# A two-layer graph network on one Trainium2 core: 128-row indirect transfers with three skipped rows in place of 125-row ones

## The reference

```
    h = jnp.maximum(_layernorm(x, axis=-1), 0.0)
    x = x + _L0_gnn_ref(h, edge_attr_2, weight, root_w, root_b, edge_index)
    h = jnp.maximum(_layernorm(x, axis=-1), 0.0)
    x = x + _L1_gnn_ref(h, edge_index, W_gat, att_src, att_dst, ...)

    # L0: messages = einsum('ek,ei,kio->eo', basis, x[row], weight)
    #     out = zeros.at[col].add(messages) / max(degree, 1) + x @ root_w.T + root_b
    # L1: alpha = leaky_relu(a_src[src] + a_dst[dst]); softmax over each dst, self loop included
    #     out = segment_sum(xp[src] * attn, dst).mean(heads) + bias
    #     h = layer_norm(out + x); layer_norm(relu(h @ w1 + b1) @ w2 + b2 + h)
```

## Time and profile before

| | us |
|---|---|
| median of 3 runs | 3408.22 (3392.78 to 3413.61) |
| the profiled execution, own time | 3399.81 |
| its span | 3398.0 |
| POOL busy | 2533.3 (75%) |
| PE busy | 2270.3 (67%) |
| DVE busy | 1842.4 (54%) |
| ACT busy | 862.2 (25%) |

### The profile page before, as it was taken

One profiled execution on the slowest core, in us unless ns is written; L12 is line 12 of the kernel. 1 busy time (PEld: TensorE's weight loads), 2 busy tenths in 40 slices (PEclk: granted clock), 3 DMA queues, 4 the chain that ended last, 5 costly groups with the idle time before them and its releaser, 6 DMA issues.

```text
span 3398.0 us, 34863 instructions
## 1 busy us (share of the span) xinstructions
PE 2270.3 (67%) x10329; PEld 1608.8 (47%) x10329; DVE 1842.4 (54%) x3167; ACT 862.2 (25%) x1636; POOL 2533.3 (75%) x2011
## 2 busy tenths in 40 slices
PE   2886777747777777777777475566561587887750
PEld 1554455535555555565555354445440244454430
DVE  4788878883433434333333232322248998797730
ACT  1332222212333232322323122222221122222220
POOL 7788888887887878787777787887840038888877
PEclk9888888877888787777877676676665798787775
DMA  2322222221111112121111111111100001111100
GB/s 57 85 70 70 68 71 65 48 63 31 33 38 35 38 37 41 36 41 35 38 27 32 26 24 24 24 27 20 23 16 0 30 15 29 32 26 28 33 10 10
DMA packets 116073, 123.70 MB, mean 36 GB/s; under 512 B 70597, under 2 KB 72618, under 8 KB 115941
## 3 DMA queue, kind: packets, MB, share of 16 engines
q0 software_dynamic: 64000, 30.57, 9.4%
q1 hardware_dynamic: 51940, 91.52, 8.4%
HBM read 59.51 MB, written 64.00 MB: 36 GB/s over the span
## 4 chain that ended last, share of the span: by engine, by line
POOL 65%; issue 19%; DVE 8%; PE 7%; DMA 0%; DVEq 0%; ACT 0%; POOLq 0%; ACTq 0%
POOL ring L409 44%; POOL x_table L431 14%; POOL out_rows L457 6%; DVE region L1457 2%; PE V L773 1%; PE C L525 1%; PE V L513 1%; DVE region L1449 1%; DVE region L1123 1%; DVE region L1433 1%; DVE region L1385 0%; PE C L773 0%; DVE region L1408 0%; DVE region L1405 0%; PE C L519 0%
## 5 line engine op out<-in xcount | busy, mean ns | idle before, releaser
L409 POOL DMA_INDIRECT ring<-in_x,index x800 | 1042.6, 1303 | 244.3 <-issue 244.0
L457 POOL DMA_INDIRECT out_rows<-ring,index_out x400 | 510.0, 1275 | 370.3 <-DVE ring L1264 250.6
L1092 DVE TENSOR_REDUCE var<-sq 125x16 f32<-125x512 f32 x325 | 220.4, 681 | 839.9 <-ACT sq L838 734.9
L409 POOL DMA_INDIRECT ring<-x_table,index x400 | 492.0, 1230 | 124.4 <-issue 124.1
L431 POOL DMA_INDIRECT x_table<-region,index_out x400 | 485.7, 1214 | 121.9 <-issue 121.9
L838 ACT ACTIVATE sq<-C 125x512 f32<-125x512 f32 x300 | 179.4, 598 | 961.9 <-PE C L525 416.5
L513 PE MATMUL V<-xT,w_q 128*128 128x500 f32 x600 | 365.3, 762 | 53.5 <-ACT xT L830 25.7
L474 PE MATMUL T<-ident,hrow 125*128 125x125 f32 x1000 | 196.3, 335 | 194.4 <-DVE hrow L1108 171.8
L525 PEld LDWEIGHTS C<-w_c,hid 128*125 128x125 f32 x2400 | 320.1, 219 | 0.0
L525 PE MATMUL C<-w_c,hid 128*125 128x32 f32 x2400 | 319.4, 296 | 0.0
L489 PE MATMUL C<-center,xT 128*125 128x128 f32 x1400 | 258.6, 347 | 78.5 <-DVE hrow L1114 47.2
(11 more groups left out here) (223 smaller groups left out, 3421.6 us busy)
## 6 DMA issues: line engine op xcount, KB each, us to landing
ring<-in_x,index POOLq DMA_INDIRECT x800
nodes<-in_x SPq DMA_DIRECT2D x25, 500.0 KB
x_table<-nodes SPq DMA_DIRECT2D x25, 500.0 KB
x_plain<-nodes SPq DMA_DIRECT2D x25, 500.0 KB
nodes<-x_plain SPq DMA_DIRECT2D x50, 250.0 KB
out_rows<-nodes SPq DMA_DIRECT2D x50, 250.0 KB
x_table<-region,index_out POOLq DMA_INDIRECT x400
ring<-x_table,index POOLq DMA_INDIRECT x400
```

Of the source, the lines that this page charges most:

```text
L409: pool.indirect_dma_start(out=ring[0:P, j, s * F:(s + 1) * F], out_offset=None, in_=table, in_offset=bass.IndirectOffsetOnAxis(ap=index[0: ...
L457: pool.indirect_dma_start(out=out[:, :], out_offset=bass.IndirectOffsetOnAxis(ap=index_out[0:P, j, s:s + 1], axis=0), in_=ring[0:P, j, s * ...
L1092: v.tensor_reduce(unit(var, k), slots(squares(k)), AX.X, ALU.add).then_inc(var_ready, 1)
```

## The change

Every indirect transfer now covers ROWS = 128 partitions. The last three rows of `index` and `index_out` are set to N = 100,000 by DVE at the start, and the gathers get the bounds check of the scatters, with `last_row` = N - 1: a row whose number is beyond it is skipped. Rows 125 to 127 of `ring` hold the bias; their load is moved from the end of SP's boot loads to their front, so N_BOOT falls by one. SP waits for DVE's two memsets before its first index load, and POOL waits for the bias before its first gather. DVE also clears rows 96 to 127 of the part of `region2` from which the scatters of `scatter_x1` now read three rows more.

```diff
-N_BOOT = 6 * 4 + 2 + 2 + 2 + 4
+N_BOOT = 6 * 4 + 2 + 2 + 2 + 3
...
+ROWS = 128
...
+            sp.dma_start(ring[P:128, :, :].rearrange("a j (s f) -> a (j s) f", f=F),
+                         root_b.rearrange("(a b f) -> a b f", a=1, b=1).to_broadcast([128 - P, NJ * CE, F])).then_inc(root_b_in, 16)
+            sp.wait_ge(index_set, 2)
             for j in range(NJ):
                 index_load(src, 0, j, None)
...
-            load(ring[P:P + 1, :, :].rearrange("a j (s f) -> a (j s) f", f=F),
-                 root_b.rearrange("(a b f) -> a b f", a=1, b=1).to_broadcast([1, NJ * CE, F]))
...
                     pool.indirect_dma_start(
-                        out=ring[0:P, j, s * F:(s + 1) * F], out_offset=None, in_=table,
-                        in_offset=bass.IndirectOffsetOnAxis(ap=index[0:P, j, s:s + 1], axis=0)).then_inc(ring_dma[j], 16)
+                        out=ring[0:ROWS, j, s * F:(s + 1) * F], out_offset=None, in_=table,
+                        in_offset=bass.IndirectOffsetOnAxis(ap=index[0:ROWS, j, s:s + 1], axis=0),
+                        bounds_check=last_row, oob_is_err=False).then_inc(ring_dma[j], 16)
...
+            pool.wait_ge(root_b_in, 16)
             gather_phase(x[:, :], 0, 0)
...
-                        out=x1_table[:, :], out_offset=bass.IndirectOffsetOnAxis(ap=index_out[0:P, j, s:s + 1], axis=0),
-                        in_=rows_out[0:P, j, s * F:(s + 1) * F], in_offset=None,
+                        out=x1_table[:, :], out_offset=bass.IndirectOffsetOnAxis(ap=index_out[0:ROWS, j, s:s + 1], axis=0),
+                        in_=rows_out[0:ROWS, j, s * F:(s + 1) * F], in_offset=None,
                         bounds_check=last_row, oob_is_err=False).then_inc(rows_landed[j], 16)
...
+            pool.wait_ge(index_set, 2)
...
-                            out=out[:, :], out_offset=bass.IndirectOffsetOnAxis(ap=index_out[0:P, j, s:s + 1], axis=0),
-                            in_=ring[0:P, j, s * F:(s + 1) * F], in_offset=None,
+                            out=out[:, :], out_offset=bass.IndirectOffsetOnAxis(ap=index_out[0:ROWS, j, s:s + 1], axis=0),
+                            in_=ring[0:ROWS, j, s * F:(s + 1) * F], in_offset=None,
                             bounds_check=last_row, oob_is_err=False).then_inc(ring_dma[j], 16)
...
+            v.memset(index[96:128, :, :], N).then_inc(index_set, 1)
+            v.memset(index_out[96:128, :, :], N).then_inc(index_set, 1)
+            v.memset(region2[96:128, 5904 + KS * GF:2 * H * TE + NJ * W], 0.0)
```

More of the change, by code:

```diff
@@ L195, in gnn_program @@
         VE = [V[0], V[1], C[1], T[1]]
+        index_set = sem("index_set"); root_b_in = sem("root_b_in")
         edges_in = sem("edges_in"); ends_in = sem("ends_in")
```

## The result

The changed kernel took **4504.05 us** (median of 4 runs, 4474.84 to 4532.82), the kernel before 3401.25 us in the same comparison (4 runs, 3392.78 to 3413.61): a ratio of 1.324, with an interval of 1.314 to 1.334. It is a third slower. The prediction said 2990 us, and its range ended at 3390.

The account below looks back on a forecast made before the run. POOL's indirect transfers were taken to bound the kernel outside the softmax stage. Gains of 66 + 165 + 92 + 97 - 2 = 418 us from the median of 3408 gave 2990 us, range 2770 to 3390.

Parts of the forecast that it names:

- Rival C: All 2,000 transfers: POOL's time goes with the rows, three more cost 29 ns, +58 us; 3468 us, chance 9%.
- Layout of the transfers: Each 125-row transfer runs on 5 engines with 25 rows each; 128 rows would spread evenly over 16, 8 each.
- Time of a transfer: POOL's indirect transfers: 0.98 us each, a saving of 0.23 us, with the 0.30 us gap unchanged.
- The check costs nothing, 26 us to both sides: Bounds check on 1,200 gathers: taken as free, with 1,200 x 0.022 = 26 us either way.
- Start-up: Boot loads: bias load and memset waits delay the first gather by 2 us, bound +5; -2 us in the sum.
- Landing: Gathered rows: spread over 16 engines they land sooner, a few us at most; nothing was taken.
- First pass: First source gather: a block falls from 133.2 to 116 us, DVE's 109.8 being the limit; 66 us in all.
- Second pass: Destination gather and table scatter: 720 transfers x 0.23 = 165 us; a block becomes 203 us, above PE's 178.
- Third pass: Second source gather: 400 x 0.23 = 92 us; a block becomes 105 us, far above PE's 77.
- Output pass: Output scatter: blocks fall to 112 us, saving 50 us, plus 47 us in the last stretch; together 97 us.
- POOL's backlog: Last stretch of output scatters: 113 left instead of 124, at 1.26 us; 142 instead of 189 us, saving 47 us.
- Rival A: Transfers of 0.85 us or less: POOL stops being the bound and other engines' floors decide; 2790 us, chance 17%.

Follow-up runs that it names:

- plain128: Changed kernel with no check and no skipped row in its 1,200 gathers, bias from its own tile; 4619.03 us, ratio 1.356, on chip 6.
- gathers128_b: Changed kernel with its 800 scatters back at 125 rows, repeated on chip 14: 3947.78 us, ratio 1.162; the same kernel took 3252.05 us on chip 4.
- rows120: Kernel before with 120-row indirect transfers, the last five of 125 rows left out, no check in the gathers: 3191.67 us.
- rows112: Kernel before with 112-row indirect transfers, rows 112 to 124 left out, no check in the gathers: 3171.21 us on chip 10.
- rows100: Kernel before with 100-row indirect transfers, the last 25 rows left out, no check in the gathers: 3208.09 us.
- skip112: Changed kernel with 112-row transfers whose last four rows are skipped, in all five passes: 3189.68 us on chip 4, 3171.86 us on chip 10.

## Why the prediction was wrong

**The step that failed** is one that the prediction did not have. It went through POOL, DVE, PE and the landings as if a signal from PE always arrived at once, and no rival had PE's increments late. In its terms, the delay of a signal was put at nothing, without a row for it. The trace of before has one late increment of 1,665, by 1.1 us, so no row there would have priced it. What the runs showed in its place: 283 of 1,545 late, 1,658 us together, and 1,323 us between the two times of the same program. Rival C, the only one on the slower side, ended at 3468 and for another reason. The forecast's own terms add up to 418 us, so no error in one of them could have made the kernel a third slower.

What is shown: the loss follows the chip or the circumstances there, and not the program alone; on such a chip it follows the passes with 128-row transfers; it comes with PE's increments that are recorded, and acted on, mostly some us and up to 31 us late (single ones 45 and 59, in plain128 and gathers128_b). What is not: why they are late, and what differs in the chips. Nor is it shown that the loss would be there without the profiler: every execution on record is one with the profiler's span and clock, and the traces on chips of the first sort also lack records. Some 41,000 to 41,600 semaphore updates are recorded on chips 4, 5 and 10, but 14,781 of the changed kernel's on chip 14, 14,434 on chip 6 and 14,295 in the first result, and 32,459 in the trace of the kernel before, whose chip has no number. The missing records keep to the same passes as the late increments (gathers128_b: 4,288 updates recorded in the slow first pass, 6,062 in the output pass; on chip 5 10,664 and 7,726). Whether both have one cause is not shown.

**Against a chip of the second sort** the forecast's steps can be judged one by one; there it came to 217 us of gain (3398.31 to 3181.21, one execution) instead of 418.

*Layout of the transfers: right.* The band from 512 B to 2 KB holds 81,713 - 50,830 = 30,883 packets, 2,021 before, and at 2 KB and above are 34,507, hardly more than SyncE's own 34,375. 16 packets of 8 rows took the place of five of 25. The kernel with 100 rows has 81,565 - 61,514 = 20,051 packets in that band and the one with 112 rows 81,565 - 51,174 = 30,391, some 10 and 15 a transfer. The trace's packet records, counted by size, say so directly. In every kernel here the software queue has 64,000 packets, 32 a transfer, and half of them are of 4 bytes. The commonest of the other 32,000, 16 a transfer:

| kernel | packets x bytes | reading |
|---|---|---|
| before | 6,052 x 3,200; 22,022 x 100 | 5 packets of 25 rows, 11 of 25 entries of 4 bytes |
| after | 19,846 x 1,024; 3,076 x 652 | 16 packets of 8 rows; in one of them 3 of the 8 are skipped |
| rows120 | 19,846 x 1,024; 2,378 x 32 | 15 packets of 8 rows, one of 8 entries |
| rows112 | 21,484 x 896 | 16 packets of 7 rows |
| rows100 | 12,796 x 1,280; 12,242 x 40 | 10 packets of 10 rows, 6 of 10 entries |

The rest are smaller than the full packet by 124 bytes for each row that is skipped (900, 776, 652 in after, where plain128, which skips none in its 1,200 gathers, has 1,200 fewer of 652 bytes and as many more of 1,024). The records name no engine: that the 16 packets of a transfer are those of 16 engines is my reading here as in the prediction. No row of before shows the 8 rows of the longest share, from which the 0.98 us is worked out; the runs showed them.

*Time of a transfer: right.* 0.98 us was forecast; 0.997 to 1.000 for gathers and 0.982 for scatters were measured, with the gap still 0.30 (366.7 us of "issue" ahead of 1,164 gathers). It came from two terms that nearly cancel: the layout alone gives 1212 - 944 = 268 ns a gather (plain128), and the check takes 53 to 60 of them. "The check costs nothing, 26 us to both sides" was mis-sized: it is 1,200 x 0.055, about 66 us. That the scatters with their check were faster than gathers without was no evidence for a free check.

*Start-up: right.* The first gather moved from 4.46 to 6.2 us; +2 was forecast. SyncE's loads from 35.79 to 51.21 us of before, the weights and the bias rows, take it 0.25 to 0.61 us each, 0.42 in the median.

*Landing: sooner, as said.* From the start of a transfer's issue to the end of its last packet it is 2.36 us before and 2.11 after on chip 5 in the median, so the rows land 0.25 us sooner, of which POOL's own 0.21 us is most.

*First pass: right in the block, too small in the sum.* A block fell from 134 to 117 us (116 forecast). POOL sets it, and not DVE: 80 x 1.30 us, and 13 us that some gathers take longer, are 117 (in the first 400 gathers these come to 47 us, 45 of them in gathers that overlap a scan of DVE), and POOL's wait for slots that PE frees did not come (2.7 us in the whole run). So POOL's saving of 0.21 us came back for its 480 gathers in this pass, 99 us with the later start taken off: 51 in the three blocks as forecast, 34 in the two blocks of gathers ahead of them, where I took 15, and 15 in the 80 that stand ahead of the first scatter, where I took nothing.

*Second pass: the step that failed on the chips of the second sort.* 165 us were forecast, and the pass took 1106 us instead of 1100. The prediction took PE's 178 busy us a block as the floor and 240 us, POOL's, as what the block takes. How far the compute engines are is told by what DVE does last for each chunk: it copies the indices, and POOL needs that copy before the 16 scatters. The 25 copies (first and last start), before and then after on chip 5:

```profile
L1323 DVE COPY index_out<-scatter_to x25: 161/164/535, 769.1 to 1873.1; 125x16 int32 x20, 125x16 int32<-125x16 int32 x5
```

```profile
L1332 DVE COPY index_out<-scatter_to x25: 163/164/224, 696.1 to 1784.6; 125x16 int32 x20, 125x16 int32<-125x16 int32 x5
```

The first scatter of the last chunk in each, and POOL's waits for these copies in the pass on chip 5:

```profile
1874.72 1.19 POOL L431 DMA_INDIRECT x_table<-region,index_out  x1 [0.30 <-issue]
```

```profile
1785.53 0.98 POOL L436 DMA_INDIRECT x_table<-region,index_out  x1 [32.24 <-DVE index_out L1332]
```

```profile
POOL x_table L436 <- DVE index_out L1332: 159.7, 20, 32.2
```

From the first copy to the last the compute engines need 1104 us before and 1089 after: 230 and 227 us a block, whatever POOL does. Before, POOL's own block was 245 us, so the copies ran ahead of it, by 32 us at the first chunk and by 89 at the 21st; then the last 80 scatters, which have no gathers between them, caught up at 24 us a chunk, and the last chunk's scatters began 1.4 us behind its copy. The pass ended where the compute engines ended, though POOL never waited. After, a block of POOL is 227 us instead of 245, which saves 71 us over four blocks; the last 80 scatters now wait for each copy and take 200 us instead of 123, which gives 76 back. So the floor of this pass is the turn that PE, ACT and DVE need together, 227 us a block where 203 was forecast, and the prediction took the busy time of the busiest for it. Eight other kernels on chips 4, 5 and 10 agree: 1094 to 1136 us in this pass, with gathers from 0.93 to 1.27 us. Which handover within the turn sets the 227 us is open.

*Third pass: right.* 92 us forecast, 89 measured (612 to 523), a block of 105 us.

*Output pass: too large.* 97 us forecast, 38 measured (635 to 597). From the first scatter to DVE's last write of the ring it is 521 us before (2763.5 to 3284.8) and 521 after (2582.5 to 3103.5), so the blocks gave nothing where 50 was forecast: that DVE and PE with 104.5 and 102.6 us busy would get a block down to 112 was the same error as in the second pass. All of the gain is POOL's backlog. It fell nearly as forecast; DVE writes the ring last 76 us ahead of the end, where 70 was said and 113 had been:

```profile
3103.53 0.69 DVE L1273 TENSOR_TENSOR ring<-nodes,hrow 125x512 f32<-125x512 f32 x1
```

The terms with what they measured: 99 - 6 + 89 + 38 - 1 for the softmax stage = 219 us, beside 217 between the medians. Of the 199 that 219 lacks to 418 the second pass has 171 and the output pass 59, and the first gave 33 back.

Rival A (POOL stops being the bound) was right in its mechanism for one pass: POOL stops leading in the second. Its price there, -225, fell with the same floor.

## What to carry to other kernels

The row count of an indirect transfer is worth a try: the change to 128 rows, in 16 packets of 8 where 125 lay in 5 of 25, took 0.21 us off a gather for POOL here, and on chips 4, 5 and 10 the kernels gained by it. Time such a change on more than one chip before believing either sign, and look whether a wait on "remote" in a one-core program is a signal that arrived late, as the 998 us of ACT here, and not work. When the leading engine gets faster, take as floor of a stage the turn that the other engines need together, which the busy share of the busiest does not tell. That the leader never waits proves no slack either: look how long each handover had been ready when the leader took it, above all the last one of the stage.

## What was not expected of the hardware

- **Late increments of PE.** On chips 6 and 14 and in the first result PE's semaphore increments came late, most by a few us and some by up to 31 (59 in gathers128_b), while 128-row indirect transfers ran: 283 of 1,545 in after, none of 1,877 for the same program on chip 5; 4500 against 3181 us. Of ACT's none is late and of DVE's 9, in five traces. 91 of the 283 are recorded within 0.2 us of another of PE's updates. With 125-row scatters on such a chip six come 1.2 to 1.8 us late, and the output pass takes 635 us in the same execution that took 1023 in its first. All of this is seen with the profiler running.
- **More rows took POOL less time.** 933 ns for 112 rows, 944 for 128, 982 for 120, 1009 for 100, 1212 for 125, all gathers without a check.
- **A bounds check on a gather costs POOL 53 to 60 ns**, skipped rows nothing (988 ns with four of them, 989 without).
- **Chips of one sort differ by less than 0.6%** (3189.68 and 3171.86 us for skip112; 3358.67 and 3360.87 for the scatters alone), so a difference of a third is not the usual scatter between chips.
